# One-hots of the node sums made by ScalarE from absolute differences, instead of by VectorE's comparison

## What is computed

```
e   = edge_feats @ W_e + b_e            # 200000 x 64 @ 64 x 128
m   = relu(e + x[src])                  # one row gathered per edge
agg = segment_sum(m, dst)               # the node sums
h   = agg + (1 + eps) * x
z   = relu(batchnorm(h @ W1 + b1));  x = layernorm(x + z @ W2 + b2)
```

## Time and profile before

| | us |
|---|---|
| median of 3 runs (3316.0 to 3318.71) | 3316.06 |
| the profiled execution | 3318.06 |
| its span, first to last instruction | 3316.0 |
| span covered by the first stage (from the start to the last add, L1324) | about 2330 |

### The profile page before, as it was taken

The page is one execution under the profiler, slowest core; times in us unless marked ns, Lnnn a source line. Parts: engine busy times, 40 slices in busy tenths (PEclk is TensorE's granted clock), DMA queues, the critical chain, the costliest instruction groups (busy, mean ns, idle before and its releaser), DMA issues.

```text
span 3316.0 us, 43422 instructions
## 1 busy us (share of the span) xinstructions
PE 2553.0 (77%) x13276; PEld 2027.6 (61%) x13276; DVE 2434.4 (73%) x4267; ACT 1579.0 (48%) x2894; POOL 1551.6 (47%) x1687
## 2 busy tenths in 40 slices
PE   4677677676677677776777767667799999999998
PEld 3555555555555555555555555555578888888887
DVE  6887887777777777777777777778679884445554
ACT  3444544444444444444444444454455555445444
POOL 6676666666666666666666666664200000000111
PEclk7777877777777777778777787777889999999999
DMA  5344333333333333333333333333233333333442
GB/s 178 104 117 149 112 112 110 110 110 110 110 110 112 112 112 112 110 113 111 110 110 110 110 111 113 115 108 99 88 119 143 123 134 138 129 134 145 154 174 81
DMA packets 157585, 394.57 MB, mean 119 GB/s; under 512 B 36944, under 2 KB 100587, under 8 KB 151979
## 3 DMA queue, kind: packets, MB, share of 16 engines
q1 hardware_dynamic: 104620, 278.06, 22.4%
q0 software_dynamic: 51008, 105.74, 14.0%
q10 hardware_dynamic: 1728, 7.92, 0.6%
HBM read 286.78 MB, written 104.80 MB: 118 GB/s over the span
## 4 chain that ended last, share of the span: by engine, by line
DVE 41%; PE 30%; another core or an unknown queue 16%; issue 7%; ACT 3%; DMA 1%; DVEq 1%; ACTq 0%; POOL 0%; SPq 0%; POOLq 0%
DVE z L1312 17%; PE psE L1145 13%; PE psA L1145 12%; DVE work L1294 5%; DVE held L1306 5%; DVE work L1319 5%; DVE work L1320 4%; DVE onehot L1300 3%; PE psE L445 2%; ACT z L863 1%; PE psA L1020 1%; DMA work<-in_edge_cols 1%; PE psA L1100 1%; ACT z L855 1%
## 5 line engine op out<-in xcount | busy, mean ns | idle before, releaser
L785 POOL DMA_INDIRECT work<-in_x_flat,idx x1563 | 1494.2, 956 | 797.7 <-issue 422.1
L855 ACT ACTIVATE z<-psA 128x490 int32 x392 | 224.0, 571 | 1214.1 <-PE psA L1020 834.8
L1312 DVE TENSOR_SCALAR z<-iota_r,key,scale 128x490 bf16<-128x490 f16 x1568 | 716.3, 520 | 3.1 <-issue 2.6
L445 PE MATMUL psE<-we,work 128*128 128x256 f32 x1564 | 665.7, 570 | 12.1 <-issue 9.9
L442 PE MATMUL psE<-edge_bias,ones_b 128*128 128x512 bf16 x391 | 222.7, 569 | 488.4 <-DMA work<-in_edge_cols 338.3
L445 PEld LDWEIGHTS psE<-we,work 128*128 128x128 f32 x1564 | 466.8, 299 | 158.1 <-issue 68.7
L1004 PE MATMUL psS<-onehot,work 128*128 128x72 f32 x3126 | 416.1, 284 | 132.2 <-issue 84.3
L1004 PEld LDWEIGHTS psS<-onehot,work 128*128 128x128 f32 x3126 | 392.3, 200 | 168.5 <-issue 158.8
L1020 PE MATMUL psA<-z 128*128 128x245 bf16 x3136 | 447.6, 293 | 55.5 <-issue 54.8
L863 ACT ACTIVATE z<-iota_c,low 128x128 bf16<-128x128 f16 x1568 | 476.8, 389 | 0.0
L1145 PE MATMUL psE<-wide,halves 128*128 128x500 f32 (+1 forms) x2058 | 448.7, 375 | 5.8 <-ACT halves L947 5.4
(11 more groups left out here) (176 smaller groups left out, 2247.9 us busy)
## 6 DMA issues: line engine op xcount, KB each, us to landing
counts<-adjacency SPq DMA_DIRECT2D x36, 3062.5 KB, 10.0
adjacency<-work SPq DMA_DIRECT2D x392, 245.0 KB
work<-in_edge_cols SPq DMA_DIRECT2D x196, 256.0 KB
work<-in_x_flat,idx POOLq DMA_INDIRECT x1563
counts<-adjacency SPq DMA_DIRECT2D x3, 1592.5 KB, 6.3
acc<-in_x_cols ACTq DMA_DIRECT2D x1, 3136.0 KB
xn<-in_x_rows SPq DMA_DIRECT2D x1, 3136.0 KB
x_spill<-xn SPq DMA_DIRECT2D x12, 256.0 KB, 2.2
```

The lines of the kernel that those rows point to most:

```text
L445: mm = pe.matmul(psE0[0:n, 2 * q:2 * q + 2, :].rearrange("p j f -> p (j f)"), eaT[:, slot, q, 0:n], we[:, :], start=False, stop=True, skip ...
L785: gp.indirect_dma_start(gath[:, g % R, j, :], None, x_flat[:, :], bass.IndirectOffsetOnAxis(ap=idx[:, g, j:j + 1], axis=0)).then_inc(rows_ ...
L855: act.activation(taken[:, w % TAKEN, :, :], ring[:, bass.ds(at, 2 * HC)].rearrange("p (a n) -> p a n", a=ODD), ACT.Copy).then_inc(evac_ok, 1)
L1312: ve.tensor_scalar(hot[:, k % RB, :], iota_r[:, :, 0:2 * HC // ODD], key[:, k:k + 1], scale[:, k:k + 1], ALU.is_equal, ALU.mult).then_inc( ...
```

## The change

`window_hot` moves from VectorE's list to ScalarE's. Instead of one comparison of `rel` and `iota_w`, ScalarE makes |rel - iota| column by column (eight instructions of 72 elements, the bias a column of `rel`), and then max(1 - that, 0) over all 576 elements in place. It waits for itself between the two (`far_ok`). The one-hots of group s+2 are made at the end of ScalarE's iteration s, one step earlier than before; VectorE's `window_held` still waits for `hot_ok`. `rel_done` tells ScalarE that `rel` is complete.

```diff
             act.activation(acc[:, 0, 0:NP], acc[:, 0, 0:NP], ACT.Copy, scale=one_eps[:, 0:1]).then_inc(agg0_ok, 1)
-            rectify(0)
+
+            def window_hot(g):
+                if g >= 2:
+                    act.wait_ge(win_mm, g - 1)
+                for j in range(J):
+                    ins = act.activation(onehot[:, g % 2, j, :], iota_w[:, :], ACT.Abs, bias=rel[:, g, j:j + 1], scale=-1.0)
+                ins.then_inc(far_ok, 1)
+                act.wait_ge(far_ok, g + 1)
+                act.activation(onehot[:, g % 2, :, :], onehot[:, g % 2, :, :], ACT.Relu, bias=1.0, scale=-1.0).then_inc(hot_ok, 1)
...
             act.wait_ge(lows_in, 1)
+            act.wait_ge(rel_done, 1)
+            window_hot(0)
+            rectify(0)
             for s in range(2):
                 low_hots(s)
+            window_hot(1)
             act.wait_ge(tab_in, 48)
             for s in range(G):
...
                 evacuate(HQ * s + 1, at[1])
+                if s + 2 < G:
+                    window_hot(s + 2)
             rectify(G - 1)
...
             ve.wait_ge(step, steps[0])
+            ve.engine_nop().then_inc(rel_done, 1)
...
-            def window_hot(g):
-                n = P
-                if g >= 2:
-                    ve.wait_ge(win_mm, g - 1)
-                ve.tensor_tensor(onehot[0:n, g % 2, :, :], rel[0:n, g, :].unsqueeze(2).to_broadcast([n, J, W]),
-                                 iota_w[0:n, :].unsqueeze(1).to_broadcast([n, J, W]), ALU.is_equal).then_inc(hot_ok, 1)
...
             add_rows(0)
-            window_hot(0)
...
                         add_rows(s + 1)
-                    window_hot(s + 1)
```

More of the change, by code:

```diff
@@ L245, in build @@
         rel_ok = sem("rel_ok")
+        rel_done = sem("rel_done")
         deg_out = sem("deg_out")
@@ L259, in build @@
         msg_ok = sem("msg_ok")
+        far_ok = sem("far_ok")
         hot_ok = sem("hot_ok")
```

## The result

| kernel | median, us (20 runs each) | ratio to before, 95% interval |
|---|---|---|
| before | 3316.32 | |
| changed | 3320.86 | 1.0014 [1.0008, 1.0020] |

A forecast was written before the change was run, and what follows sets the result against it. The prediction took each step's add to wait for the window's signal, not VectorE's work. From 3318.06 us, -1 (last steps) and +1 (start) gave 3318 us profiled, 3317 us for the median; range 3288 to 3345.

The forecast's parts named there:

- In the 158 steps that wait, it is worth 0.: VectorE's freed 0.66 us a step only lengthens its wait before the add, from 2.7 to about 3.4 us.
- What the add waits for: VectorE's add waits for the window's signal `win_mm`; GpSimd's eight gathers or TensorE's step share its 11.67 us rhythm.
- Nine instructions come to ScalarE: ScalarE's new one-hot work takes 2.7 us a step, with ends of 2.4 and 4.2 us.
- The 660 us in the last part of the prediction: Expected rise of ScalarE's busy time, from 196 x (8 x 0.34 + 0.65).
- Price 0: ScalarE's added work costs nothing, since it idles 6.27 us in an ordinary step.
- The tail, -1 us: Last steps of the first stage, without waits: three comparisons saved there are 2 us; taken as -1, ends 0 and -25.
- ScalarE becomes late: Rival: in short steps the rectification behind the new one-hots delays the window; slower, 3343 us, chance 0.17.
- The start, +1 us: ScalarE makes two groups' one-hots before its first step, 5.4 us, mostly covered by idling; +1 us, ends 0 and 5.4.
- The gathers: Rival: GpSimd's gathers set the pace and the comparison held them; 19 us gain, 3298 us, chance 0.08.
- the long gather did not lengthen its step: Argument from one gather of 1.34 us, against a median of 0.944, whose step still took 11.69 us.
- VectorE's time counts: Rival: the 38 steps that don't wait keep their gain, 3292 us, or every step does, 3188 us; chance 0.15.

The follow-up runs named there:

- A: Group of runs in which the kernel before, measured beside each, takes 3315 to 3316 us; the changed kernel's ratio there is 1.0014.
- B: Group of runs in which the kernel before, measured beside each, takes 3349 us; leaving the comparison out gave ratio 0.9997 there.
- C: Group of runs in which the kernel before, measured beside each, takes 3005 us; the changed kernel took 2979.21 us there, ratio 0.9916.

## Why the prediction held, and where its terms were off

The forecast was no change, 3317 us and a range of 3288 to 3345; it came to 3320.86. Step by step:

- **"In the 158 steps that wait, it is worth 0."** Right in A and B: 515.1 us of wait against the 507 forecast, and 0.9994 and 0.9997 without any comparison.
- **What the add waits for.** The prediction left it between the gathers and TensorE's way through a step. It is the gathers: two fewer bring the step from 11.8 us (B) to 9.2, where VectorE's own 9.0 begins, and an earlier edge load brings nothing. And it isn't GpSimd's own time but the signal of the window, which the burst of gathers holds.
- **"Nine instructions come to ScalarE", 2.7 us.** Measured 2.77 in the step shown, and 2108.3 - 1579.0 = 529 us in all, 2.70 each. The 660 us in the last part of the prediction added overlapping durations; by its own 2.7 it should have said 529. VectorE's busy time fell by 2434.4 - 2318.9 = 115.5, not 147: the same mistake, since by its own 0.66 us it should have said 129; the rest isn't accounted for.
- **"Price 0" for ScalarE's work.** Mis-sized: in B it grows to 4.8 us between the twenty-sixth and the 191st add, 0.03 us a step; in A some 3 to 4 us are inferred from the medians and the steady steps, not seen. No row of before could show this.
- **The tail, -1 us.** The sign was wrong, by its own rival "ScalarE becomes late": 2 us are won by the missing comparison and all of it is lost where VectorE waits 2.97 and 0.80 us for the one-hots, 35.4 us before and 35.9 after.
- **The start, +1 us.** The first add was 4.7 us late, within its ends, but 25 steps later 0.2 us was left of it, and with the old start the kernel is no faster.
- **What was luck.** The prediction was worked out from a profile of A and met A. In C the same change gives 0.9916, by the rival to which the prediction gave 0.08, and nothing in its rows told that such a case exists.
- **The rivals.** "The gathers" is true in C, 26 us for its 19: the order of size was right, and the argument against it ("the long gather did not lengthen its step") was right only where the window's signal is held. "ScalarE becomes late" is true where steps get short, in the tail and with four gathers. "VectorE's time counts" wasn't seen anywhere: where VectorE was made the bound, the loop through ScalarE took its place.

## What to carry to other kernels

Before an engine is relieved, ask whether it waits in every round: here the freed time was wait within 8 us of the forecast. Then ask which engine comes next when the wait is gone, and whether the new home of the work lies in the loop of waits: moved into an in-order list between a copy that waits for TensorE and a sum that VectorE's add stands behind, 2.7 us cost more than the 0.66 us it saved. And the same change had a ratio of 1.0014 in one group of runs and of 0.9916 in another: a "remote" wait on the critical path, one for which the profile names no instruction, need not be there the next time, so the kernel before has to be measured and looked at beside every run.

## What was not expected of the hardware

- The same kernel takes 3316, 3349 or 3005 us, and what makes the difference isn't known. In the first two groups the semaphore that TensorE raises at the end of a window shows 8.7 us after the product, 11.44 us (A) or 11.62 us (B) after the first of eight gathers; in the third 0.01 us after it. Steps are 11.7, 11.8 and about 10 us. What delays the signal isn't known; that it goes with the number of gathers (8.82 us for six in B) is shown.
- A GpSimd gather of 950 ns is 16 ns longer on average in C (9 ns in A) when a comparison with two SBUF operands runs in each step. It counts (25 us) only where gathers follow each other without a wait.
